# Graph attention on one Trainium2 core: messages and nodes' scores of the last attention as a rounded high part and an exact rest

## The reference, cut to what matters

```
xh = (x @ W).reshape(N, H, D)
a_src = jnp.einsum('nhd,hd->nh', xh, att_src)
a_dst = jnp.einsum('nhd,hd->nh', xh, att_dst)
e = jax.nn.leaky_relu(a_src[src] + a_dst[dst], NEG_SLOPE)
m = jax.ops.segment_max(e, dst, num_segments=N)
e = jnp.exp(e - m[dst])
denom = jax.ops.segment_sum(e, dst, num_segments=N)
alpha = e / denom[dst]
msg = xh[src] * alpha[:, :, None]
out = jax.ops.segment_sum(msg, dst, num_segments=N)
```

## Time and profile before

| | |
|---|---|
| device time, median of 3 runs | 6355.63 us |
| the profiled execution, first to last instruction (span) | 5104.4 us |
| mean granted TensorE clock, share of full | 0.883 |
| last attention, first gather to last store issue | 4129.2 to 4734.0 us |
| PE / DVE / ACT / POOL busy over the whole span | 80% / 52% / 34% / 49% |
| the same in 4300 to 4400 us, within the last attention | 79% / 48% / 32% / 79% |

### The profile page before, as it was taken

The page is one execution under the profiler, slowest core; times in us unless marked ns, Lnnn a source line. Parts: engine busy times, 40 slices in busy tenths (PEclk is TensorE's granted clock), DMA queues, the critical chain, the costliest instruction groups (busy, mean ns, idle before and its releaser), DMA issues. The chain is left out here.

```text
span 5104.4 us, 77209 instructions
## 1 busy us (share of the span) xinstructions
PE 4099.5 (80%) x21807; PEld 3218.8 (63%) x21859; DVE 2678.9 (52%) x5664; ACT 1722.8 (34%) x3861; POOL 2494.7 (49%) x2520
## 2 busy tenths in 40 slices
PE   7886169879999994599959999847999858877178
PEld 6664057758888882366648888736777646666055
DVE  7788276568888884300024444424333545555553
ACT  5564023113333331121216666523333313333032
POOL 0075657645555553677757666440000067776400
PEclk9988579989999995699979999978999977788579
DMA  1075346589999993100027777611000046666300
GB/s 41 7 228 160 86 145 201 181 268 333 335 332 332 333 324 98 53 17 16 16 73 228 219 221 225 190 55 59 0 0 0 23 129 197 194 198 195 111 13 25
DMA packets 606663, 747.83 MB, mean 147 GB/s; under 512 B 139329, under 2 KB 529148, under 8 KB 602493
## 3 DMA queue, kind: packets, MB, share of 16 engines
q0 software_dynamic: 118624, 306.99, 20.1%
q1 hardware_dynamic: 321239, 264.48, 17.3%
q10 hardware_dynamic: 166630, 174.25, 10.9%
HBM read 488.05 MB, written 257.44 MB: 146 GB/s over the span
## 5 line engine op out<-in xcount | busy, mean ns | idle before, releaser
L1756 POOL DMA_INDIRECT a_far<-kv_table,a_index x416 | 469.5, 1129 | 411.8 <-DVE a_index L1909 311.4
L2327 POOL DMA_INDIRECT fl_far<-x_table,fl_index x416 | 419.0, 1007 | 226.4 <-issue 122.5
L2062 POOL DMA_INDIRECT a_far<-src_table,a_index x416 | 452.4, 1088 | 132.3 <-issue 124.4
L1259 POOL DMA_INDIRECT by_dst<-dst_row,place x416 | 409.5, 984 | 211.2 <-issue 109.5
L1259 POOL DMA_INDIRECT by_src<-src_row,place x416 | 409.5, 984 | 148.7 <-issue 115.0
L2364 PE MATMUL ps<-fl_w,fl_hid 128*128 128x256 f32 x1664 | 395.1, 380 | 0.5 <-ACT fl_hid L2430 0.5
L1783 PE MATMUL ps<-a_w,a_edge_t 128*128 128x256 f32 x1664 | 394.9, 380 | 0.0
L3024 POOL DMA_INDIRECT starts<-p_near,p_at x25 | 24.3, 973 | 708.3 <-DMA starts<-p_zero 693.2
L2364 PEld LDWEIGHTS ps<-fl_w,fl_hid 128*128 128x128 f32 x1664 | 314.9, 191 | 48.2 <-ACT fl_hid L2430 0.9
L1783 PEld LDWEIGHTS ps<-a_w,a_edge_t 128*128 128x128 f32 x1664 | 301.1, 191 | 32.6
L910 ACT ACTIVATE f_hid<-ps,f_bn 128x320 f32<-128x320 f32 x320 | 197.5, 617 | 327.9 <-PE ps L864 327.9
(11 more groups left out here) (484 smaller groups left out, 9779.6 us busy)
## 6 DMA issues: line engine op xcount, KB each, us to landing
partial<-a_out ACTq DMA_DIRECT2D x208, 546.0 KB, 6.7
a_edge<-by_dst SPq DMA_DIRECT2D x104, 516.0 KB, 6.5
partial_f<-fl_out ACTq DMA_DIRECT2D x26, 2056.0 KB
dst_row<-in_edge_attr SPq DMA_DIRECT2D x52, 1024.0 KB
xn_sb<-q_table SPq DMA_DIRECT2D x416, 128.0 KB
fl_keys<-key_rows SPq DMA_DIRECT2D x26, 1024.0 KB, 5.4
a_keys<-local_rows SPq DMA_DIRECT2D x104, 128.0 KB
f_w<-in_L_ffn_W SPq DMA_DIRECT2D x4, 2048.0 KB, 12.2
```

Of the source, the lines that this page charges most:

```text
L1259: self.nc.gpsimd.indirect_dma_start(out=self.table, out_offset=bass.IndirectOffsetOnAxis(ap=self.place[:, n:n + 1], axis=0), in_=self.row[ ...
L1756: gathered[b % 4].count(nc.gpsimd.indirect_dma_start(out=far[:, b, u, :], out_offset=None, in_=kv_table, in_offset=bass.IndirectOffsetOnAx ...
L2062: gathered[b].count(nc.gpsimd.indirect_dma_start(out=far[:, b, u, :], out_offset=None, in_=src_table, in_offset=bass.IndirectOffsetOnAxis( ...
L2327: gathered[q * 4 + t // 4].count(nc.gpsimd.indirect_dma_start(out=far[:, q, t, :], out_offset=None, in_=table, in_offset=bass.IndirectOffs ...
```

## The change

The matrix `same` is written as float32r, a form of float32 that TensorE takes in one pass. A float32r operand is rounded, so each other operand is split in two: a rounded high part, and the rest, the operand less its high part. Two float32r products that accumulate in PSUM stand for one float32 product.

- At the start VectorE waits for `first_loaded`, copies `first` into `first_high` (3328 columns), subtracts into `first_low`, and only then goes on to the memset and the first indices. TensorE waits for `first_split` in place of `first_loaded`.
- Each of the 4 products L2101 becomes two, with `first_high` and `first_low`; each of the 4 products L2116 becomes two, with `msg_high` and `msg_low`.
- ScalarE, after it has placed the weights of quarter k-6, waits for the messages of that quarter and for its own placing, and copies 4 x 264 columns into `msg_high` (`high_made`). The rest of its step is queued behind this.
- VectorE at step k first waits for `high_made` of quarter k-6 and subtracts 4 x 264 columns into `msg_low` (`low_made`). The index, `same` and all else of the step are queued behind this. Its loop now runs with the lag `SUM`; a new flag keeps the messages themselves at the lag `MSG`.
- TensorE waits for `low_made` in place of `msg_ready` and `weight_placed`.

```diff
--- before.py
+++ after.py
@@ -2010,15 +2010,17 @@
         tops = st.sb("tops", [P, 2, CT, HEADS])
         centre = st.sb("centre", [P, CT, HEADS])
         weight = st.sb("weight", [P, 2, CT, HEADS])
-        same = st.sb("same", [P, BODY, 4, P])
+        same = st.sb("same", [P, BODY, 4, P], F32R)
+        first_high, first_low = st.sb("first_high", [P, ETILES, HEADS], F32R), st.sb("first_low", [P, ETILES, HEADS], F32R)
         msg = st.sb("msg", [P, 2, 4, SEG])
+        msg_high, msg_low = st.sb("msg_high", [P, 2, 4, SEG], F32R), st.sb("msg_low", [P, 2, 4, SEG], F32R)
         out = st.sb("out", [P, 2, 4, ROW])
         gathered = [st.moved(k, QUARTERS // BODY * 4) for k in range(BODY)]
         stored = [st.sem("stored0"), st.sem("stored1")]
         names = ("chain", "first_loaded", "noted", "indexed", "pool_passed", "near_ready", "raw_made", "scored", "heads_noted", "turned", "node_copied",
-                 "top_ready", "top_turned", "centred", "weighed", "weight_placed", "marked", "keys_turned", "same_made", "msg_ready", "summed", "copied")
+                 "top_ready", "top_turned", "centred", "weighed", "weight_placed", "marked", "keys_turned", "same_made", "msg_ready", "first_split", "high_made", "low_made", "summed", "copied")
         (chain, first_loaded, noted, indexed, pool_passed, near_ready, raw_made, scored, heads_noted, turned, node_copied,
-         top_ready, top_turned, centred, weighed, weight_placed, marked, keys_turned, same_made, msg_ready, summed, copied) = map(st.sem, names)
+         top_ready, top_turned, centred, weighed, weight_placed, marked, keys_turned, same_made, msg_ready, first_split, high_made, low_made, summed, copied) = map(st.sem, names)
 
         SCORES, NODES, TOPS = (ps[:, 0, k * P:(k + 1) * P] for k in range(3))
         KEYS, SUMS, NEAR = (1, 2), (4, 6), ps[:, 3, 0:4 * HEADS]
@@ -2076,7 +2078,7 @@
                         last = nc.tensor.transpose(ps[:, KEYS[b % 2], u * P:(u + 1) * P], node[:, b, u:u + 1].broadcast_to([P, P]), ident)
                     last.then_inc(keys_turned, 1)
 
-                pe.wait_ge(first_loaded, 16)
+                pe.wait_ge(first_split, 1)
                 turn_keys(0, 0)
 
                 def quarter(i, b, scores, sums):
@@ -2098,8 +2100,9 @@
 
                             pe.wait_ge(raw_made, i * BODY + b)
                         for u in range(4):
-                            last = nc.tensor.matmul(NEAR[:, u * HEADS:(u + 1) * HEADS], same[:, b, u, :],
-                                                    first[:, bass.ds(i * (4 * BODY) + b * 4 + u, 1), :], start=True, stop=True)
+                            for part in (first_high, first_low):
+                                last = nc.tensor.matmul(NEAR[:, u * HEADS:(u + 1) * HEADS], same[:, b, u, :],
+                                                        part[:, bass.ds(i * (4 * BODY) + b * 4 + u, 1), :], start=(part is first_high), stop=(part is first_low))
                         last.then_inc(near_ready, 1)
                     for v in range(2):
                         if v == 1 and c is not None:
@@ -2108,12 +2111,13 @@
                             nc.tensor.transpose(TOPS, down[:], ident).then_inc(top_turned, 1)
                         if sums:
                             if v == 0:
-                                pe.wait_ge(msg_ready, m + 1 + BODY)
-                                pe.wait_ge(weight_placed, m + 1)
+                                pe.wait_ge(low_made, m + 1)
 
                             pe.wait_ge(copied, m * 2 + v + 1)
                             for t in range(2):
-                                last = nc.tensor.matmul(ps[:, SUMS[v] + t, 0:SEG], same[:, s, v * 2 + t, :], msg[:, s % 2, v * 2 + t, :], start=True, stop=True)
+                                for part in (msg_high, msg_low):
+                                    last = nc.tensor.matmul(ps[:, SUMS[v] + t, 0:SEG], same[:, s, v * 2 + t, :], part[:, s % 2, v * 2 + t, :],
+                                                            start=(part is msg_high), stop=(part is msg_low))
                             last.then_inc(summed, 1)
                 run(pe, SUM, quarter)
 
@@ -2143,6 +2147,10 @@
 
                             act.wait_ge(weighed, i * 2 + (b - SUM) // 4 + 1)
                         nc.scalar.copy(msg[:, s % 2, :, D:SEG], weight[:, s // 4, at, :]).then_inc(weight_placed, 1)
+
+                        act.wait_ge(msg_ready, m + 1 + BODY)
+                        act.wait_ge(weight_placed, m + 1)
+                        nc.scalar.copy(msg_high[:, s % 2], msg[:, s % 2]).then_inc(high_made, 1)
 
                         act.wait_ge(stored[s % 2], (i * 4 + (b - SUM) // 2) * 16 + 16)
                         nc.scalar.copy(out[:, s % 2, :, SEG:ROW - 1], tops[:, s // 4, at, :]).then_inc(marked, 1)
@@ -2169,6 +2177,10 @@
             def _(dve):
                 ch = Chain(dve, chain)
                 dve.sem_inc(msg_ready, BODY)
+                dve.wait_ge(first_loaded, 16)
+                ch.link(nc.vector.tensor_copy(first_high[:], first[:]))
+                ch.link(nc.vector.tensor_tensor(first_low[:], first[:], first_high[:], ALU.subtract))
+                dve.sem_inc(first_split, 1)
                 ch.link(nc.vector.memset(fresh[:], 0.0))
 
                 def take_index(i, b):
@@ -2184,12 +2196,18 @@
                     nc.vector.tensor_tensor(same[:, b], ps[:, KEYS[b % 2], :].rearrange("p (u e) -> p u e", u=4),
                                             node[:, b].unsqueeze(2).broadcast_to([P, 4, P]), ALU.is_equal).then_inc(same_made, 1)
 
-                def quarter(i, b, scores, sums):
+                def quarter(i, b, scores, lows):
                     m = i * BODY + b - MSG
                     s = (b - MSG) % BODY
                     c = chunk_before(i, b)
                     h = (b // 4 - 1) % 2
                     k = i * BODY + b
+                    sums = not isinstance(i, int) or 0 <= m < QUARTERS
+                    if lows:
+
+                        dve.wait_ge(high_made, m)
+                        half = (b - SUM) % 2
+                        nc.vector.tensor_tensor(msg_low[:, half], msg[:, half], msg_high[:, half], ALU.subtract).then_inc(low_made, 1)
                     if not isinstance(i, int) or k + AHEAD < QUARTERS:
                         take_index(i + (b + AHEAD) // BODY, (b + AHEAD) % BODY)
                     if scores:
@@ -2230,7 +2248,7 @@
 
                 for b in range(AHEAD):
                     take_index(0, b)
-                run(dve, MSG, quarter, lambda: ch.loop(BODIES - 2, 2 * (1 + 4 + 2)))
+                run(dve, SUM, quarter, lambda: ch.loop(BODIES - 2, 2 * (1 + 4 + 2)))
 
 
 def filter_stage(core, name, edge_rows, key_rows, table, wf1, bf1, wf2, bf2, partial):
```

## The result

The changed kernel takes 6588.94 us in the median (6581.59 to 6602.25), the kernel before 6356.93; the ratio is 1.0371, 95% interval 1.0349 to 1.0393. That is 232 us more, where 323 were forecast. Both differences are far outside the noise.

What follows compares the result with a forecast made beforehand. POOL's gathers bound the kernel; the change closes a chain of 8.79 us a quarter (7.21 at full clock). Weighted nine to one, +339 and +179 give +323: 6355.6 + 323 = 6679, say 6680 us, range 6610 to 6740 (outer 6490 to 6740).

Steps and rivals of the forecast that it cites:

- rival 2: Mid-stage of the last attention: the chain closes but TensorE keeps its full clock, +179, 6535 us; chance 0.20.
- the term that failed: Whole program: the runs' median lies 1251.2 us above the span of before, carried over unchanged.
- the signs named: First gather about 4141.6, POOL idle behind VectorE, high-copy wait some 3 us, clock 0.5 to 0.6, quarter 8.8 us.
- The links: Successive parts of one mid-stage quarter, from low subtraction to next low: 8.59 us at lower clock, 7.01 at full.
- the steps that begin a chunk: Once in four quarters exponential, key copy and transpose join the chain: 0.8 us, 0.2 a quarter, making 8.79.
- rival 4: TensorE's sums: a float32r product still takes two passes, about 8.2 us a quarter, +280, 6635; chance within the forecast's 0.62.
- The clock: TensorE in the last attention: busy 49%, so at the lower clock for nine tenths of the stage.
- the forecast's mixture: Last attention: nine parts lower clock (+339 us) to one part full clock (+179), giving +323.
- the first row: Earlier trace, 4130 to 4160, only transposes and score products: TensorE busy 62% of the time, granted clock 0.50.
- The head: Start of the last attention: landing, copy and subtraction delay the first gather by 12.5 us, bounds 6.9 to 14.1.
- POOL as the bound (+49): Last attention: chain shorter than added up, POOL stays the bound; head 12.5 and held gathers 37, 6405 us; chance 0.10.
- TensorE as the bound: Mid-stage: TensorE sets the pace, cheaper sums save 83 us less the 12.5 head, 6285; chance 0.03 including other gains.

Runs made afterwards that it cites:

- lag 7: Changed kernel with sums one quarter later (TensorE sums quarter k-7) and `msg_low` made after the messages: 5147.68 us, 44.8 over the kernel before, ratio 1.0082.

## Why the prediction was right, and where it was off

The sign, the bound and the mechanism are those of the forecast. The 6589 us lie in the outer range (6490 to 6740), but not in the forecast's own (6610 to 6740); they lie where the prediction had put rival 2, full clock, and the traces show that it isn't rival 2. That they lie in a range at all is luck, since none was made wide for what moved the number (the term that failed, below).

**The bound and the sign.** POOL set the pace and the change closed a chain through four engines. Shown twice over: moving one instruction gives 234 us back, and doubling one link adds its length to each quarter, 110 us. Of the signs named, every one came in kind, but for the name of POOL's releaser in the page; that POOL waits for VectorE is read from the timeline.

**The links,** forecast and measured in the quarter shown: low to `same` 1.37, 1.25; `same` to score products 0.73, 0.83; score products to first sum 1.73, 1.73; to the first copy 1.27, 1.26; between the copies 0.89, 0.88; to the placing 1.18, 1.19; to the high copy 0.25, 0.25; high copy and wait 1.17, 1.10 (the copy itself 1.07, as forecast). Sum 8.59, 8.49. With the steps that begin a chunk 8.79 was forecast and 8.60 measured: of the 0.8 us put down for them about 0.4 lay on the chain. Pairs of the sums are 0.22 us apart at the lower clock, half of what float32 took, so that one pass is one pass and rival 4 falls:

```profile
5707.16 0.42 PE L2119 MATMUL ps<-a_msg_high,a_same 128*128 128x264 f32 x1
...
5707.38 0.42 PE L2119 MATMUL ps<-a_msg_low,a_same 128*128 128x264 f32 x1
```

**The clock.** Granted 0.55 to 0.59, 0.5 to 0.6 forecast; rival 2 falls. That the clock was a term is shown by the products added to no purpose. The clock's 0.57 didn't shorten the quarters by a tenth of the difference, as the forecast's mixture had it: eight in ten are between 8.31 and 8.75 us. The way to the clock, by the share of time that TensorE is busy, was right here and isn't a guide: with lag 7 TensorE is busy 76% to 81% and is granted 0.53 to 0.57, at about the share at which the kernel before has 0.80. For the same reason the first row is a weak sign for what the prediction takes from the Trainium skill ("TensorE: Matmul & The Clock Gate", Part 4) on transposes, since here a stretch full of products is granted nearly as little.

**The head.** 12.6 us against 12.5; its copy took 1.89 and its subtraction 3.63 us (1.98 and 3.6).

**The rivals.** POOL as the bound (+49) is what the kernel with lag 7 is: 44.8 with the head and the held gathers. It was wrong for this order, since the chain did close. TensorE as the bound had no support: POOL waited for nobody before, and with lag 7 TensorE's cheaper sums save nothing.

**The term that failed** is the last line of the sum: "The runs' median is 1251.2 above the span of before, and I carry that over unchanged." No run shows such a constant beside the program: the changed kernel's span is 1.8 us short of its run, so that the run behind the trace of before took some 5106 us, and the median of 6355.63 was taken where the program takes longer. Where the trace fits the runs, the forecast of +323 met +327; where it didn't, +232. The 91 us between 323 and 232 go with this mismatch, but which stage they lie in, and why, stays open.

**Luck.** That +323 comes so near the later +327 is in part luck. The links at the lower clock alone gave +339, with 0.19 us a quarter too much for the chunk steps, 18 us in 98 steps. The tenth of full clock, which the trace doesn't show, took 16 off again. In the traces of like span the stage grew by 320 us, from 606 in the mean of three to 926.

## What to carry to other kernels

When a change puts a new producer between two engines, write down for one iteration which instruction each engine has queued behind the wait, and follow it until you come back to the start. If the walk closes within one iteration, its length is the new period, if it is longer than what bound the loop before, whatever the busy shares say, and the cure is to let the consumer lag by one more iteration. And set a trace's span against the run times before using both: if they differ by more than a few us, they don't speak of the same conditions, and a difference taken from one need not hold for the other.

## What the runs showed of the hardware

A VectorE copy of 3328 columns from SBUF to SBUF (1.89 us, some 0.57 ns a column, half of what the subtraction takes) held up a gather that had already begun, 2.40 us in place of 1.00; this is one case. The subtraction and the message product held up only gathers that started within them: the gather of 4128.79 finished inside the subtraction's first 0.1 us, and the one of 4131.50 waited for its end. The Trainium skill ("SBUF — State Buffer", Who interferes with whom) has the two cases apart, copies in a two-port mode and instructions with two SBUF inputs, and that both block a gather agrees with these durations. It also says that whoever issues first gets the shared ports for the whole instruction, and there the trace differs: the gather had begun 0.39 us before the copy and was held all the same, while the copy took the 1.89 us that it takes with no gather beside it. And it reports a probe in which `tensor_tensor` did not stall DMA, where the subtraction here held a gather for 3.1 us.

Added matrix work made the kernel 80 us faster: at 75% busy TensorE was granted 0.83, at 56% it was granted 0.57. But the busy share alone doesn't tell the clock. With `msg_low` after `same` TensorE was 72% to 74% busy and was granted 0.57 to 0.60, with lag 7 76% to 81% and 0.53 to 0.57; the kernel before had 0.80 to 0.81 at 79% to 81%. The two at the lower level do their sums in float32r, the other two have long float32 products, the sums or the added ones. No run here takes these apart.
